# Scores of four heads at once in the last self attention of a four-part attention chain

## The reference, cut to what matters

```python
def _mha(q_in, kv_in, wq, bq, wk, bk, wv, bv, wo, bo):
    q = (q_in @ wq.T + bq).reshape(b, -1, HEADS, HD).transpose(0, 2, 1, 3)
    k = ...; v = ...
    scores = jnp.einsum('bhqd,bhkd->bhqk', q, k) * HD ** (-0.5)
    p = jax.nn.softmax(scores, axis=-1)
    o = jnp.einsum('bhqk,bhkd->bhqd', p, v)
    return o.transpose(0, 2, 1, 3).reshape(b, -1, WIDTH) @ wo.T + bo
...
    h = _layernorm(x, ln1_g, ln1_b)
    x = x + _mha(h, h, sa_wq, ...)
```

## Time and profile before

| what | us |
|---|---|
| median of 3 runs | 4755.02 (4749.33 to 4756.09) |
| the profiled execution: its own time | 4757.91 |
| its span, first to last instruction | 4756.1 |
| PE busy | 3922.0 (82%) |
| DVE busy | 3115.8 (66%) |
| ACT busy | 2330.0 (49%) |
| POOL busy | 2116.6 (45%) |
| mean granted TensorE clock | 0.938 |

### The profile page before, as it was taken

How to read it: one execution, slowest core, us unless ns; L and a number is a source line. 1 busy time by engine, 2 the same in 40 slices (tenths; PEclk the granted TensorE clock), 3 DMA queues, 4 the chain that set the end, 5 groups by cost and what they waited for, 6 DMA issues and landing times. The chain is left out here.

```text
span 4756.1 us, 51594 instructions
## 1 busy us (share of the span) xinstructions
PE 3922.0 (82%) x16584; PEld 2005.4 (42%) x16584; DVE 3115.8 (66%) x4144; ACT 2330.0 (49%) x4397; POOL 2116.6 (45%) x2146
## 2 busy tenths in 40 slices
PE   6987897798799668888788878887788768889897
PEld 3443343344344324444444444444444434444343
DVE  2543263263335249999899989999899956474553
ACT  2321331232233147776677767776677634343342
POOL 0210020031012047787778867787788833132231
PEclk9998999899899879999999999999999979899999
DMA  3000000000000043222333223222332210000000
GB/s 136 1 1 11 0 1 5 6 1 0 11 1 1 24 116 93 84 67 80 88 87 94 84 80 98 80 67 80 94 95 80 61 57 1 10 1 11 1 6 5
DMA packets 132058, 215.91 MB, mean 45 GB/s; under 512 B 18960, under 2 KB 118544, under 8 KB 124496
## 3 DMA queue, kind: packets, MB, share of 16 engines
q1 hardware_dynamic: 131504, 201.08, 14.7%
q0 software_dynamic: 288, 11.53, 0.6%
HBM read 186.26 MB, written 26.30 MB: 45 GB/s over the span
## 5 line engine op out<-in xcount | busy, mean ns | idle before, releaser
L1612 POOL TENSOR_TENSOR m_db<-m_u,m_bb 128x512 f32<-128x512 f32 (+1 forms) x1280 | 1465.0, 1163 | 456.2 <-DVE m_hh L1564 453.5
L1564 DVE TENSOR_TENSOR_SCAN m_hh<-psum,m_kept,m_db 128x512 f32<-128x512 f32 (+1 forms) x1024 | 1195.0, 1200 | 30.3 <-POOL m_u L1657 17.5
L1363 ACT ACTIVATE psum<-m_dt,m_am 128x512 f32<-128x512 f32 (+1 forms) x1280 | 818.4, 644 | 410.2 <-DVE m_hh L1564 406.5
L1291 PE MATMUL psum<-cst,m_hh 128*128 128x128 f32 x4608 | 665.0, 285 | 325.4 <-DVE m_yt L1578 214.5
L1291 PEld LDWEIGHTS psum<-cst,m_hh 128*128 128x128 f32 x4608 | 525.0, 145 | 761.5 <-DVE m_yt L1578 427.1
L1301 PE MATMUL psum<-m_ys,cst 128*128 128x512 f32 x1024 | 550.5, 620 | 0.0
L651 POOL TENSOR_SCALAR a_pr<-a_pr,a_ri 128x512 f32<-128x512 f32 x256 | 173.9, 692 | 683.9 <-DVE a_ri L593 683.9
L1578 DVE SCALAR_TENSOR_TENSOR m_yt<-psum,m_bc,m_yt 128x512 f32<-128x512 f32 x600 | 436.7, 728 | 55.8 <-PE psum L1291 54.7
L651 POOL TENSOR_SCALAR c_pr<-c_pr,c_ri 128x512 f32<-128x512 f32 x256 | 173.9, 692 | 437.3 <-DVE c_ri L593 437.3
L1375 ACT ACTIVATE m_ys<-psum,m_bc 128x512 f32<-128x512 f32 x512 | 343.9, 672 | 26.5 <-PE psum L1291 25.5
L513 POOL TENSOR_TENSOR a_pr<-a_pr,a_ri 128x512 f32<-128x512 f32 x64 | 66.5, 1042 | 624.8 <-DVE a_ri L481 624.8
(11 more groups left out here) (222 smaller groups left out, 5907.9 us busy)
## 6 DMA issues: line engine op xcount, KB each, us to landing
m_bb<-b_rows SPq DMA_DIRECT2D x48, 1024.0 KB, 4.7
m_xr<-x_line SPq DMA_DIRECT2D x128, 192.0 KB, 3.6
m_bb<-b_rows SPq DMA_DIRECT2D x32, 768.0 KB, 4.3
m_xr<-x_line SPq DMA_DIRECT2D x128, 160.0 KB, 3.4
m_xr<-x_line SPq DMA_DIRECT2D x128, 128.0 KB, 3.0
m_xr<-x_line SPq DMA_DIRECT2D x128, 96.0 KB, 3.1
a_w1b<-w1b_in POOLq DMA_DIRECT2D x1, 7168.0 KB, 29.2
x_line<-m_xc SPq DMA_DIRECT2D x32, 192.0 KB, 4.4
```

The costliest lines, as they stand in the source:

```text
L1291: mm = nc.tensor.transpose(s[:, e * P:(e + 1) * P], hh[:, n % 2, e, t * P:(t + 1) * P], ident)
L1363: nc.scalar.activation(bank(DECAY[u % len(DECAY)])[:, 0:w], dt[:, g % 2, e, 0:w], ACT.Exp, scale=am[:, layer_of(g) % 2, e * DS + n:e * DS ...
L1564: nc.vector.tensor_tensor_scan(hh[:, n % 2, e, 0:w], bank(DECAY[u % len(DECAY)])[:, 0:w], db[:, u % 4, 0:w], kept[:, n, e:e + 1] if g % NI ...
L1612: nc.gpsimd.tensor_tensor(db[:, u % 4, 0:w], us[:, g % 2, e, 0:w], bb[:, at % 2, n % 4, 0:w], ALU.mult).then_inc(pool_done, pr.pool.step(f ...
```

## The change

The last self attention gets functions of its own. A plan `QuadPlan` makes units in fours: four heads of one query block, which lie in four different groups of 32 rows. The scores of a quad are four matmuls one behind the other, with one semaphore step after the last. Banks: the scores take 1 to 5 in turn, the sums bank 0 alone, the flips 6 and 7 as before. `Ring` now keeps the emptied marks by bank for the whole program of the part, since banks 0 and 1 have several users. Each unit has a maximum of its own (128x512), and an exp waits for the maximum of its own unit. ACT now copies every second flipped unit, DVE the others. The software pipeline goes over quads: PE flips quad i-1 right behind the scores of quad i, and weighs a block in every second step. The instructions of a unit are otherwise the same; the first self attention of the program (L1) keeps its functions.

```diff
@@ Ring
     def take(self, job, steps, emptied):
-        k = self.i % len(self.slots)
+        k = self.slots[self.i % len(self.slots)]
         self.i += 1
-        freed, self.last[k] = self.last[k], (steps.sem, steps.at(emptied))
-        self.prog.where[job] = self.slots[k]
-        return self.view(self.slots[k]), freed
+        freed, self.prog.emptied[k] = self.prog.emptied.get(k), (steps.sem, steps.at(emptied))
+        self.prog.where[job] = k
+        return self.view(k), freed
+class QuadPlan:
+    def unit(self, u):
+        heads, half, _, _ = self.blocks[u // 8]
+        return heads[u % 4], 2 * half + u // 4 % 2
+    def by_act(self, u):
+        return u % 2 == 0
...
+                self.sums, self.five = Ring(prog, bank, [0]), Ring(prog, bank, [1, 2, 3, 4, 5])
...
+            def pe_quads(self, pe, name, q, k_of, v_of, plan):
+                def scores(i):
+                    units = range(4 * i, 4 * i + 4)
+                    found = [self.five.take(f"{name} s {u}", p.act, f"{name} exp {u}") for u in units]
+                    for _, emptied in found:
+                        if emptied:
+                            pe.wait_ge(*emptied)
+                    for u, (b, _) in zip(units, found):
+                        h, qt = plan.unit(u)
+                        rows, tile, keys = k_of(h)
+                        mm = nc.tensor.matmul(b, q[rows, tile, qt * P:(qt + 1) * P], keys, start=True, stop=True)
+                    mm.then_inc(pe_done, p.pe.step(f"{name} s {i}"))
...
+                for i in range(plan.n + 2):
+                    if i < plan.n:
+                        scores(i)
+                    if 1 <= i <= plan.n:
+                        for u in range(4 * i - 4, 4 * i):
+                            flip(u)
+                    if i >= 3 and i % 2 == 1:
+                        weigh((i - 3) // 2)
+            def dve_quads(self, dve, name, plan, dst, bias):
+                def maximum(u):
+                    dve.wait_ge(pe_done, p.pe.at(f"{name} s {u // 4}"))
+                    if u >= 8:
+                        dve.wait_ge(act_done, p.act.at(f"{name} exp {u - 8}"))
+                    nc.vector.tensor_reduce(self.nm[:, u % 8:u % 8 + 1], self.full(f"{name} s {u}"), AX.X, ALU.max,
+                                            negate=True).then_inc(dve_done, p.dve.step(f"{name} max {u}"))
...
+                for i in range(plan.n + 2):
+                    if i >= 1 and i <= plan.n:
+                        inverse(2 * i - 1)
+                    if i < plan.n:
+                        for u in range(4 * i, 4 * i + 4):
+                            maximum(u)
+                    if 1 <= i <= plan.n:
+                        empty(4 * i - 3)
+                    if i < plan.n:
+                        inverse(2 * i)
+                    if 1 <= i <= plan.n:
+                        empty(4 * i - 1)
+                    if i >= 4 and i % 2 == 0 and (i - 4) // 2 in plan.closing.values():
+                        output(plan.blocks[(i - 4) // 2][2])
+                output(plan.blocks[-1][2])
+            def act_quads(self, act, name, plan):
...
+                for i in range(plan.n + 1):
+                    if i >= 1:
+                        empty(4 * i - 4)
+                    if i < plan.n:
+                        for u in range(4 * i, 4 * i + 4):
+                            act.wait_ge(dve_done, p.dve.at(f"{name} max {u}"))
...
+                            nc.scalar.activation(self.pr[:, u % 6, :], self.full(f"{name} s {u}"), ACT.Exp, ...)
+                    if i >= 1:
+                        empty(4 * i - 2)
```

More of the change, by code:

```diff
@@ L154, in __init__ @@
             Steps(s, known.get(n, {})) for s, n in zip(sems, ("pe", "act", "dve", "pool")))
-        self.where = {}
+        self.where, self.emptied = {}, {}
         self.known_where = known.get("where", {})
@@ L170, in __init__ @@
     def __init__(self, prog, view, slots):
[L171 removed]
+        self.prog, self.view, self.slots, self.i = prog, view, slots, 0
     def take(self, job, steps, emptied):
[L175 removed]
+        k = self.slots[self.i % len(self.slots)]
         self.i += 1
[L177 to L179 removed]
+        freed, self.prog.emptied[k] = self.prog.emptied.get(k), (steps.sem, steps.at(emptied))
+        self.prog.where[job] = k
+        return self.view(k), freed
 class SideBanks:
@@ L239, in flipped, with __init__ @@
         return ptr[k % 2][:, i + u % 2, :, (qt % 2) * P:(qt % 2 + 1) * P]
+class QuadPlan:
+    def __init__(self, blocks):
+        self.blocks, self.n = blocks, 2 * len(blocks)
+        self.closing = {g: k for k, (_, _, g, _) in enumerate(blocks)}
+    def unit(self, u):
[3 more added lines that the diff above has]
+        return u % 2 == 0
+    def flipped(self, ptr, u):
+        return ptr[u // 8 % 2][:, u % 4, :, (u // 4 % 2) * P:(u // 4 % 2 + 1) * P]
 def build(nc, known, x_in, ctx_in, cst_in, w0_in, w1a_in, w1b_in, v0_in, w2_in, v2_in, w3_in, v3_in, out):
@@ L645, in act_self, with flip, weigh @@
                                                      ACT.Copy).then_inc(act_done, p.act.step(f"{name} flipped {u}"))
-            def pool_self(self, pool, name, plan):
+            def pe_quads(self, pe, name, q, k_of, v_of, plan):
                 p = self.prog
-                for u in range(2 * plan.n):
+                banks = {}
+                def scores(i):
[9 more added lines that the diff above has]
+                    mm.then_inc(pe_done, p.pe.step(f"{name} s {i}"))
+                def flip(u):
+                    b, emptied = self.trn.take(f"{name} t {u}", p.act if plan.by_act(u) else p.dve, f"{name} flipped {u}")
+                    if emptied:
+                        pe.wait_ge(*emptied)
+                    pe.wait_ge(pool_done, p.pool.at(f"{name} normed {u}"))
+                    for kt in range(NT):
+                        mm = nc.tensor.transpose(b[:, kt * P:(kt + 1) * P], self.pr[:, u % 6, kt * P:(kt + 1) * P],
+                                                 ident)
+                    mm.then_inc(pe_done, p.pe.step(f"{name} t {u}"))
+                def weigh(k):
+                    heads, half, g, opens = plan.blocks[k]
+                    if opens:
+                        banks[g], emptied = self.sums.take(f"{name} o {g}", p.dve, f"{name} o {g} out")
+                        if emptied:
+                            pe.wait_ge(*emptied)
+                    pe.wait_ge(dve_done, p.dve.at(f"{name} flipped {8 * k + 7}"))
+                    pe.wait_ge(act_done, p.act.at(f"{name} flipped {8 * k + 6}"))
+                    for kt in range(NT):
+                        for n, h in enumerate(heads):
+                            values, rows, first, last = v_of(h, kt)
+                            mm = nc.tensor.matmul(banks[g][rows, half * 2 * P:(half + 1) * 2 * P], values,
+                                                  self.ptr[k % 2][:, n, kt, :], start=first, stop=last)
+                    mm.then_inc(pe_done, p.pe.step(f"{name} w {k}"))
+                for i in range(plan.n + 2):
[6 more added lines that the diff above has]
+                        weigh((i - 3) // 2)
@@ new lines, in dve_quads, with inverse, empty, output @@
+            def dve_quads(self, dve, name, plan, dst, bias):
+                p = self.prog
+                def maximum(u):
[4 more added lines that the diff above has]
+                                            negate=True).then_inc(dve_done, p.dve.step(f"{name} max {u}"))
+                def inverse(j):
+                    u = 2 * j
+                    dve.wait_ge(act_done, p.act.at(f"{name} exp {u + 1}"))
+                    if j >= 4:
+                        dve.wait_ge(pool_done, p.pool.at(f"{name} normed {u - 7}"))
+                    nc.vector.reciprocal(self.rih[:, u % 8:u % 8 + 2], self.smh[:, u % 8:u % 8 + 2])\
+                        .then_inc(dve_done, p.dve.step(f"{name} inverse {j}"))
+                def empty(u):
+                    dve.wait_ge(pe_done, p.pe.at(f"{name} t {u}"))
+                    if u >= 16:
+                        dve.wait_ge(pe_done, p.pe.at(f"{name} w {u // 8 - 2}"))
+                    nc.vector.tensor_copy(plan.flipped(self.ptr, u),
+                                          self.full(f"{name} t {u}").rearrange("p (k t) -> p k t", k=NT))\
+                        .then_inc(dve_done, p.dve.step(f"{name} flipped {u}"))
+                def output(g):
+                    dve.wait_ge(pe_done, p.pe.at(f"{name} w {plan.closing[g]}"))
+                    nc.vector.tensor_scalar(dst[:, g, :], self.full(f"{name} o {g}"), bias[:, g:g + 1], None,
+                                            ALU.add).then_inc(dve_done, p.dve.step(f"{name} o {g} out"))
+                for i in range(plan.n + 2):
[13 more added lines that the diff above has]
+                output(plan.blocks[-1][2])
@@ L650, in pool_self @@
+            def pool_self(self, pool, name, units):
+                p = self.prog
```

(5 more changed lines are left out.)

27 lines of the change are left out of this document (21 added, 6 removed).

## The result

The changed kernel takes 4726.61 us, median of 5 runs (4724.83 to 4734.25), the kernel before 4755.02 (4749.33 to 4760.1) beside it. The ratio is 0.9945, with a 95% interval of 0.9932 to 0.9957: 0.55% or some 26 us faster. The profiled execution took 4731.41 us by its own clock, 26.5 less than the one of before, and its span shrank by as much.

A forecast was written before the change was run, and what follows sets the result against it. PE was taken to bound the stage, with small waits. Four stages of 98.6 us plus a 2.0 us wait made 396.4 against 415.9, 19.5 less; from the median of 4755.0 this gave 4736 us, range 4722 to 4746.

The forecast's parts named there:

- A quad costs one pair: Scores on PE: four heads on four row groups take 1.14 us, against 1.06 for a pair.
- In steady state the faster scores are worth nothing: Middle of a stage: a block takes 11.92 us against 11.88 before, PE idling 3.7 us a block instead of 1.7.
- the loop of the new order: Each step: scores, four maxima, DVE's copy of unit 4i-3, last flip; 5.03 us, or 6.89 with a weigh.
- ACT's extra copies are free: Middle of a stage: ACT's two extra copies a block lie in its idle time.
- The end: End of a stage, from the seventh weigh to the last: 5.25 us.
- The start: First scores to first weigh: 19.3 us at full clock instead of 22.9, plus 2.3 for one and a half half-clock steps.
- The rival that the half clock would stay until the first weigh: Start of a stage: half clock up to 24 us, 102.6 us a stage, 4752 us in all; chance 0.15.
- The clock in steady state: Blocks: clock falls as PE idles a third, 16.7 us a block, over 100 more; chance 0.05, shared with another loop wait.
- The new wait: First scores of stages 2 and 4 wait for DVE to empty bank 1: 1.0 us each, 2.0 in all.
- The sum: Four stages of 98.6 us plus 2.0 give 396.4 against 415.9, 19.5 less.
- 93.5 a stage: Better rival: quad 1.06, maxima 0.57, clock kept; 93.5 to 95 us a stage, 4718 to 4722 us; chance 0.12.
- 1.0 us in 60 steps: Slower rival: PE runs four heads as two pairs or singly, first maximum 1.0 us later each step, 4800 us; chance 0.08.

The follow-up runs named there:

- Experiments 1 and 2: The changed kernel with DVE's copy of unit 4i-3 moved ahead of the third maximum: 4677.56 us; the changed kernel with every quad's scores issued twice: 4776.97 us.
- Experiment 4, e3: The kernel before with ACT copying every second flipped unit instead of every fourth; 4752.81 us, ratio 0.9997.
- e10: The kernel before with a maximum for each bank, the first exp of a pair waiting for the first only; 4722.92 us, ratio 0.9929.
- e5: The changed kernel with DVE's copy after two maxima and 22 transposes added on PE between each stage's first two quads; 4677.55 us, ratio 0.9829.

## Why the prediction was right, and where it was not

It said 4736 and faster; 4726.6 lies inside the forecast's own range of 4722 to 4746. Point by point:

- **A quad costs one pair.** 1.14 forecast, 1.07 measured, against 1.06 for a pair: two more row groups cost 0.01. The estimate of 1.12 beside it took 0.86 for one matmul; the rows have 0.86 for a second pair. Reader of the scores after 1.20 (forecast 1.26), maxima 0.60 apart (0.61).
- **In steady state the faster scores are worth nothing.** Right against the order of before: the loop of the new order takes back what they give. A block of 11.92 was forecast, 11.73 came, against 11.88 before; the wait stood where it was named. Experiments 1 and 2 show it from both sides: DVE's copy moved earlier gives 1.5 us a block, slower scores cost their own length.
- **ACT's extra copies are free.** Right in the kernel after: what PE waits for is DVE, and 0.25 for ACT. Experiment 4 shows it for the old order.
- **The end.** 5.25 forecast, 5.18 measured: 15.9 us of the gain.
- **The start.** 19.3 at the full clock and 2.3 for the half clock were forecast, 21.6; 19.74 came on average. The term that was mis-sized is the half clock: 2.3 a stage, for one and a half steps at 1.5 each, that is some 7.5 us of it. Measured it costs 0.2, 1.4, 0 and 1.4 us, 3.0 in all instead of 9.2: stages 2 and 4 have 7 us of it, stage 1 has 3.5 and stage 3 none. The rival that the half clock would stay until the first weigh fell. The reason given, that four groups of 32 rows are nearer to two of 64, isn't shown: no run changes the row groups alone. What the runs show is that without a filler all ten starts with pairs at which the clock fell (before, e3, e10) had 17 to 24 us of half clock in one piece, and no start with quads had more than 7 in one piece.
- **The clock in steady state.** Here a step failed. The prediction took it as all or nothing, priced a clock that stays down at over 100 us, gave it under 0.05, and held against it one cross attention that idled more at clock 1.00. What came lies between: short falls after which the clock is back within a step, 7.6 us in all. That row spoke of another pattern of work and excluded nothing. The Trainium skill, TensorE: Matmul & The Clock Gate, section A second HAM failure mode: psum-queue depth-cycling, describes the like for a bf16 kernel that goes from PSUM bank to PSUM bank: short idle times of PE between groups of matmuls, and a clock that swings between its two levels. The trace agrees in kind (a weigh of 3.60 behind a pause of 1.48, beside 1.93), and the prediction didn't weigh it.
- **The new wait.** 2.0 us forecast; 1.22 and 1.01 came, ahead of stages 2 and 4. The row of stage 2:

```profile
4113.56 1.14 PE L681 MATMUL psum<-c_k,c_q 32*128 32x512 f32 x8 [1.22 <-DVE c_x L403]
```

- **The sum.** -19.5 was forecast and the span gave -26.5: 4.8 by the stages (start -1.9 and blocks +0.8 a stage, end -0.1), -0.2 back by the wait, 2.4 by unchanged parts of the program. Two terms were too high, the loop by 4.6 and the start by 7.4, and one was left out, the falls in the middle, 7.6: that they partly cancelled, and that the rest of the program ran 2.4 shorter, is luck. Two sums of the rivals are a little off: 93.5 a stage gives 4716 and not 4718, and 1.0 us in 60 steps gives 4796 and not 4800.

What the prediction didn't see at all is how easily the same gain was had otherwise. It read the single maxima as a cost of the new order, 2.44 against 2.28. The runs say the opposite: single maxima made the old order 34 us faster, 20 of it with the clock held, and the quads up to 10, since the consumer behind the first bank starts one bank earlier.

**What stays open.** Why the clock falls in some stages and steps and not in others with the same order: stage 3 of the kernel after kept it at its start, as did stages 2 and 4 of e10, behind equal pauses in the records. Whether the row groups or the order around them make the half clock short with quads. Whether e5's filler is worth anything. And why the unchanged parts scatter by some 18 us from one profile to another.

## What to carry to other kernels

Before making an engine faster, walk one step of the loop with every engine's own order, from each instruction to whoever waits for it: a gain on PE was lost behind one copy of DVE queued after four maxima, and moving that copy paid 49 us where the change had paid 28. Split an instruction whose first part has a waiting reader, even where the split makes it longer. And compare against a version with the clock kept up: here fourteen spare transposes a stage brought the old order as much as the whole change did.

## What the hardware showed that was not expected

- Four f32 matmuls of 32x128 by 32x512 on four row groups hold PE 1.07 us, as long as two on two groups (1.06).
- PE's clock falls to 1.2 GHz in the middle of steady work, behind pauses of no more than 1.27 to 1.48 us a step with PE busy three quarters of the time (42.08 of 57.56 us); 0.5 us of added transposes in each pause kept it at 2.4 GHz in the blocks of all four stages.
- At the start of a stage the half clock lasts 17 to 24 us in the kernel before, with PE busy nearly all the time (pairs on two groups of 32 rows; 20.00 of 20.00 us in stage 1), and 0 to 7 us in the kernel after (quads on four); the order around them differs too, so the row groups aren't shown to be the cause.
